# Loading in order of need, stacks read in two goes and another order of products in a four-layer attention and feed-forward kernel

## The chip, the cores and the metric

One core of one Trainium2 chip runs the whole program. The metric is the device time in microseconds (us) of one execution, median of the runs. The engines are TensorE (PE in the profile, with its weight loads as PEld), VectorE (DVE), ScalarE (ACT), GpSimd (POOL) and SyncE (SP), which here issues nearly all transfers.

## The reference

The input x is 4 batches of 512 tokens of 256 channels, the context is 4 batches of 512 tokens of 128 channels, all in 32-bit floats. Each of four layers adds a cross attention and then a feed-forward to x:

```python
x = x + _L0_xattn_ref(_layernorm(x), ctx_512, ...)   # 16 heads of 16: causal self part plus context part
x = x + _L0_ffn_ref(_layernorm(x), ...)              # ternary weights, gelu, 1024 hidden
x = x + _L1_xattn_ref(_layernorm(x), ctx_512, ...)   # 16 heads of 16
x = x + _L1_ffn_ref(_layernorm(x), ...)              # weights adapted by tokens
x = x + _L2_xattn_ref(_layernorm(x), ctx_512, ...)   # two blocks with 16 heads of 32, each with its own feed-forward
x = x + _L2_ffn_ref(_layernorm(x), ...)              # gated, two hidden layers of 1024, output
x = x + _L3_xattn_ref(_layernorm(x), ctx_512, ...)   # 16 heads of 16
x = x + _L3_ffn_ref(_layernorm(x), ...)              # 4-bit rounding of x, weights and hidden values
```

The last feed-forward is `nvfp4_linear(silu(gate) * up, down_w)`: its input and its hidden values are rounded in blocks of 16 to a 4-bit grid, each block with a scale of 8 bits.

## The kernel before

The program is written as a plan: one list of steps (`Turn`, `ProjectStack`, `ReadStack`, `Smax`, `GateUp` and others), in an order made by the Python code. Each engine's program walks that list and emits its own part of each step, so the place of a step in the list is its place on every engine that takes part in it, and on SP's queue. Waits are on semaphores; `hold` (`Hold`) makes the engines that it names wait for a list of events, and at the end of each stage all engines, SP too, wait for everything.

**Memory.** X (all tokens, 128 partitions by 16 tiles by 256) stays in the on-chip memory for the whole program. XT holds the normalised and transposed x, ctxT the transposed context, and xn is scratch: the normalised tiles, and in `load_context` (L878) the raw context too. PSUM has 8 banks of 128x512: three pairs `bank_t`, `bank_o` and `bank_m`. A `Banks` object (L62) hands them out in turn, and who takes one waits until its last reader is done. During attention the ring `misc` is `bank_m` alone.

**The start.** SP loads x (4 transfers, L254), the context (L886, 1 MB in runs of 512 bytes), the weights of L1's attention (L864), the biases of L0's feed-forward (L1085) and then L0's weights and biases (`L0_xattn`, L911). PE transposes the context for all four batches (`load_context`: 16 transposes, 4 copies by ACT), batch 0 of x is normalised into the same xn (`LazyNorm`, L334), transposed and copied, and `hold(loads)` (L929) waits for all of L0's loads.

**Attention with heads of 16** (L0, L1, L3; `attention`, L420). A unit is 8 heads of a batch; L0 has 16 units, L1 and L3 have 8. For each unit PE projects K and Q (`project_stack`, L510), ACT writes the result and a rounded high half, POOL the low half, SP spills both halves to DRAM and reads them back into the stacks `KS` and `QS` (`ReadStack`, L538 and L2581: 6 transfers of 128 KB for K, 6 for Q). A stack has 4 slots, one for a pair of heads. The first pass (`Smax`, L573) takes the scores of each pair `s` and each of 4 query tiles to find the row maxima on DVE; every `Smax` waits for the whole of both stacks. Then the maxima are turned, spilled and read into the stack as additional rows, and the second pass makes logits, exponentials and values. `chores` and `delayed` set what is done at each tick: `later(n, step)` delays a step by n ticks, `run_due` (L494) takes what is due and one chore. Unit 0 is prepared by `run_all()` before the first score; POOL fills rows of ones (`StackRest`, L798), and the statistics of the remaining batches (`norm.rest`, L800) are the first chore after it.

**The L2 feed-forward** (`L2_ffn`, L1438) goes over two pairs of batches. Weight blocks come in over SP two ahead of their use (`load_block`), are split by ACT and DVE (`split_block`: L2230, L2391, L2232) and used by PE; the output (`output`, L1526) takes 8 blocks of `w3` with all 8 banks. The 4-bit weights of the last layer are made in its background.

**The start of L3** (`L3_xattn`, L1579): after the stage's end SP loads the 4-bit weights, L3's attention weights and the context, PE transposes the context, DVE fills rows of ones (two memsets, L2133), makes batch 0's statistics and normalises it, after which PE transposes it and projects K and Q.

**The last stage** (`L3_ffn`, `main` at L1806) has 19 items of work: 3 for the x of batches 1 to 3, and 16 tiles of 128 tokens. In step k of its loop come, in plan order: `hidden_of(k + 2)` (`GateUp`: 4 groups of 2 matmuls into 4 banks, silu by ACT at L2408, the gating product by DVE at L2301); the turning of item k-2 (2 groups of 4 transposes, 2 copies by ACT at L2400, and for a tile the down product of 8 matmuls and DVE's addition to X at L2305); the block maxima of item k+1 (L2257); the grid of item k (L2284, L2286 on DVE, L2405 on ACT); the scales of item k+1 (9 small DVE instructions, L2551 on POOL); the rounding of item k (L2291, L2294 on DVE, L2559 on POOL). Its ring `f.ring` has 5 banks; a step takes 7. `end_step` carries the last steps of the attention along for k below 6.

Of the kernel before, what the change touches and what calls it, by code (L numbers as in the profile page):

```python
# [8 lines left out]
P = 128  # L9
# [80 lines left out]
ReadStack = namedtuple("ReadStack", "at un which spill after landing")  # L90
# [51 lines left out]
class Unit:  # L142
    def __init__(self, n, b, j, job, u, last):
        self.n, self.b, self.j, self.job, self.u, self.last = n, b, j, job, u, last
        self.buf, self.stacked, self.smax, self.m_in, self.raw_out = None, [], None, None, []

# [36 lines left out]
def build_program(nc, dram, out):  # L183
    ctx = ExitStack()
    with ctx:
# [68 lines left out]
        x_in = [load(X[:, TB * b:TB * b + TB, :], dram["x"][b].rearrange("(t p) c -> p t c", p=P)) for b in range(B)]  # L254
# [79 lines left out]
        class LazyNorm:  # L334
# [16 lines left out]
            def steps(self, b, ring, more=()):  # L351
# [3 lines left out]
                def normal():  # L355
# [4 lines left out]
                    if self.bias is not None:  # L360
                        row, e_row = self.bias
                        bias_added[b] = add_rows(X[:, TB * b:TB * b + TB, :], row, [self.normal[b], e_row])
# [57 lines left out]
        def attention(tag, scope, D, jobs, project, st, norm=None, following=None, side=None):  # L420
# [117 lines left out]
            def read_stack(un, which, written):  # L538
                if un.n >= st.n and un.n - st.n not in finished:
                    later(1, lambda: read_stack(un, which, written))  # L540
                    return
                at_ = landing(n=3 * st.q_of)
                add(ReadStack(at, un, which, split_dram[which][un.n % 3],
                              [written, stack_done.get(un.n - st.n), st.ready[un.buf]], at_))
                spill_read[which, un.n] = at_.done
                un.stacked.append(at_.done)
# [26 lines left out]
            def smax(un, s, qt):  # L573
# [3 lines left out]
                step = Smax(at, un, s, qt, tile, [*tiles.free[i_t], *un.stacked], mm,  # L577
# [218 lines left out]
            run_all()  # L796
            if D == 16:
                add(StackRest(st, st.ready, st.v_ones))  # L798
# [58 lines left out]
            tail.ot_free = OT_free  # L857
# [20 lines left out]
        def load_context():  # L878
            ctx_tok = xn[:, :, :, :].rearrange("p s t c -> p (s t c)").rearrange("p (t c) -> p t c", c=CC)
            e_in = load(ctx_tok, dram["ctx_512"].rearrange("b (t p) c -> p (b t) c", p=P), xn_free)  # L880
            for b in range(B):
                e_t, e_c = turn([ctx_tok[:, TB * b + i, :] for i in range(TB)], [e_in], "scalar", ctxT[:, b, :])
# [3 lines left out]
        ctx_ready = load_context()  # L886
# [24 lines left out]
        def L0_xattn(scope, keep, follows):  # L911
# [3 lines left out]
            W = {n: sb(scope, f"L0_{n}", [P, KC, C]) for n in ("Wq", "Wk", "Wv", "Wcq")}  # L915
            Wc = {n: sb(scope, f"L0_{n}", [P, 1, C]) for n in ("Wck", "Wcv")}
            bq = sb(scope, "L0_bcols", [P, 4, KC])
            rows = {n: sb(scope, f"L0_{n}", [P, C]) for n in ("bv", "bcv", "bp")}
# [3 lines left out]
            loads += [load(bq[:, i, :], dram[f"L0_xattn_{n}_cols"])  # L922
                      for i, n in enumerate(("bq", "bk", "bcq", "bck"))]
            loads += [row_load(rows[n], f"L0_xattn_{n}") for n in rows]
            norm = LazyNorm((rows["bp"], loads[-1]), lambda t: x_in[t // TB])
            for step in norm.steps(0, ALL):
                step()
            xt = norm.ready
            hold(loads)  # L929
            xsrc = lambda b: (XT[:, b, :, :], KC, xt[b])  # L930
            csrc = lambda b: (ctxT[:, b:b + 1, :], 1, [ctx_ready])
            return attention("L0", scope, 16, [
                dict(qsrc=xsrc, ksrc=xsrc, Wq=parts(W["Wq"]), Wk=parts(W["Wk"]), Wv=W["Wv"], bq=bq[:, 0, :], bk=bq[:, 1, :],
                     bv=rows["bv"], mode="causal"),
                dict(qsrc=xsrc, ksrc=csrc, Wq=parts(W["Wcq"]), Wk=parts(Wc["Wck"]), Wv=Wc["Wcv"], bq=bq[:, 2, :],
                     bk=bq[:, 3, :], bv=rows["bcv"], mode="full")], project_into(X, Wo), st, norm, follows)
# [148 lines left out]
        def L0_ffn(keep, side, norm):  # L1085
            b1, b2 = sb(keep, "L0f_b1", [P, KF]), sb(keep, "L0f_b2", [P, C])
            th = sb(keep, "L0f_th", [P, 2, 4])
            loads = [load(b1[:, :], dram["L0_ffn_b1_cols"]), row_load(b2, "L0_ffn_b2")]
            f = split_ffn(keep, "L0f", X, X, b2, b1, loads, side, exact=True)
            for b in range(2):  # L1090
# [1562 lines left out]
```

## Time and profile before

| | us |
|---|---|
| median of 3 runs | 3652.71 (3636.51 to 3660.86) |
| the profiled execution | 3634.89 |
| its span in the profile | 3633.1 |
| PE busy in the span | 2869.3 (79%) |
| DVE busy | 2040.3 (56%) |
| ACT busy | 1460.1 (40%) |
| POOL busy | 1146.9 (32%) |

The profile's times count from the start of the span. Busy time is the time in which an engine carried out an instruction; waits stand beside the instruction that came after them, with what released it. PEclk is the clock granted to TensorE as a share of the full clock.

### The profile page before, as it was taken

Reading aid. Unit: us, or ns where it says so; the run is one execution under the profiler, and the core shown is the slowest. Engines: PE = TensorE matmul, PEld = TensorE weight load, DVE = VectorE, ACT = ScalarE, POOL = GpSimd, SP = SyncE. Lnnn points to the kernel's source line nnn. Section 1 sums busy time; section 2 is a strip of 40 time slices with the busy share of each in tenths; the row PEclk is TensorE's granted clock in tenths of the full one; section 3 lists DMA queues with packets and bytes.
Section 4 is the critical chain, followed back from the end, with each engine's and each line's share of the span. In section 5 each row is a group of like instructions: output and inputs, shape, how many; then the busy total and the mean of one; then the engine's idle time right before and its main releaser. Section 6 shows DMA issues by size and latency. Waiting matters only on the chain. (4 is left out here: it accounts for less than half of the span.)

```text
span 3633.1 us, 44859 instructions
## 1 busy us (share of the span) xinstructions
PE 2869.3 (79%) x16756; PEld 1615.4 (44%) x16756; DVE 2040.3 (56%) x3607; ACT 1460.1 (40%) x1932; POOL 1146.9 (32%) x1007
## 2 busy tenths in 40 slices
PE   4888888658866979999866888877999997588544
PEld 2333333443324534444662344356778776233122
DVE  3445546756634735444784666685454443566587
ACT  1254555415551225444422545432433432266422
POOL 2122322221222225555413768650010110122333
PEclk7599989777886989999987899888999998699666
DMA  5355545024521001111100000000221221564100
GB/s 125 72 114 102 117 101 116 19 48 109 106 70 39 1 18 36 40 40 60 59 7 12 1 1 1 13 12 15 74 76 34 66 61 58 91 117 97 32 10 14
DMA packets 129176, 198.50 MB, mean 55 GB/s; under 512 B 35712, under 2 KB 65921, under 8 KB 128833
## 3 DMA queue, kind: packets, MB, share of 16 engines
q1 hardware_dynamic: 97216, 143.23, 17.4%
q0 software_dynamic: 31744, 52.41, 5.2%
q8 instruction: 134, 2.20, 0.3%
q14 instruction: 82, 0.66, 0.1%
HBM read 130.73 MB, written 64.75 MB: 54 GB/s over the span
## 5 line engine op out<-in xcount | busy, mean ns | idle before, releaser
L2148 DVE TENSOR_REDUCE L_mx<-bank_t 128x2 f32<-128x1024 f32 (+3 forms) x512 | 562.7, 1121 | 492.8 <-PE bank_t L1956 307.8
L2355 ACT ACTIVATE L_P<-bank_t 128x1024 f32<-128x1024 f32 (+2 forms) x512 | 477.9, 945 | 469.9 <-PE bank_t L1970 285.5
L2148 DVE TENSOR_REDUCE L2a_mx<-bank_t 128x2 f32<-128x1024 f32 x256 | 311.4, 1222 | 398.5 <-PE bank_t L1933 397.7
L2355 ACT ACTIVATE L2a_P<-bank_t 128x1024 f32<-128x1024 f32 x256 | 261.6, 1023 | 289.0 <-PE bank_t L1945 288.7
L1956 PE MATMUL bank_t<-L_KS,L_QS 48*128 48x512 f32 (+2 forms) x1024 | 261.7, 514 | 105.6 <-DMA L_QS<-L_spill_q_halves 84.8
L1970 PE MATMUL bank_t<-L_QS,L_KS 50*128 50x512 f32 (+2 forms) x1024 | 241.5, 476 | 108.2 <-DVE L_mx L2148 81.2
L1933 PE MATMUL bank_t<-L2a_QK 32*128 32x512 f32 x1536 | 255.9, 448 | 71.6 <-DVE L2a_mx L2148 35.5
L2001 PE MATMUL bank_o<-L_P,L_V 128*32 128x512 f32 (+3 forms) x2048 | 286.4, 636 | 2.6 <-ACT xn L2362 1.8
L1956 PEld LDWEIGHTS bank_t<-L_KS,L_QS 48*128 48x128 f32 x1024 | 107.5, 209 | 349.9 <-issue 246.5
L1941 PE MATMUL bank_t<-L2a_QK 32*128 32x512 f32 x1536 | 259.4, 447 | 0.0
L1933 PEld LDWEIGHTS bank_t<-L2a_QK 32*128 32x128 f32 x1536 | 138.0, 197 | 236.6 <-issue 105.5
L2470 POOL TENSOR_TENSOR L_lo<-L_full,L_hi 128x512 fp32r<-128x512 f32 x64 | 81.2, 1269 | 449.3 <-ACT L_hi L2342 429.7
L1895 PE MATMUL bank_t<-L2g_act_high,L2g_w_high 128*128 128x512 f32 x472 | 186.8, 396 | 18.8 <-DVE L2g_w_low L2232 16.6
L1970 PEld LDWEIGHTS bank_t<-L_QS,L_KS 50*128 50x128 f32 x1024 | 106.4, 207 | 204.5 <-DVE L_mx L2148 140.4
L2239 DVE TENSOR_TENSOR L2g_act_low<-ctxT,L2g_act_high 128x512 fp32r<-128x512 f32 x96 | 67.4, 703 | 218.2 <-ACT L2g_act_high L2396 218.2
L1895 PE MATMUL bank_t<-L2g_act_high,L2g_w_low 128*128 128x512 f32 x472 | 185.2, 392 | 0.0
L1895 PE MATMUL bank_t<-L2g_act_low,L2g_w_high 128*128 128x512 f32 x472 | 185.2, 392 | 0.0
L2480 POOL TENSOR_TENSOR L2a_sums<-L2a_sums,L2a_P 128x1024 f32<-128x1024 f32 x64 | 153.6, 2400 | 31.2 <-ACT L2a_P L2355 27.1
L2001 PE MATMUL bank_o<-L2a_P,L2a_V 128*32 128x512 f32 (+3 forms) x896 | 141.3, 566 | 1.7 <-ACT L2a_P L2355 1.7
L2475 POOL TENSOR_TENSOR L2a_diag<-L2a_P,after_q 128x256 f32<-128x256 f32 x128 | 94.9, 742 | 143.7 <-issue 80.8
L2005 PE MATMUL bank_o<-L2a_P,ones 128*32 128x512 f32 x512 | 138.0, 616 | 0.0
L1941 PEld LDWEIGHTS bank_t<-L2a_QK 32*128 32x128 f32 x1536 | 130.6, 195 | 13.8 <-issue 10.7
(424 smaller groups left out, 6057.6 us busy)
## 6 DMA issues: line engine op xcount, KB each, us to landing
L_KS<-L_spill_k_halves SPq DMA_DIRECT2D x192, 128.0 KB, 4.6
L_QS<-L_spill_q_halves SPq DMA_DIRECT2D x192, 128.0 KB, 5.2
L_spill_raw<-xn POOLq DMA_DIRECT2D x64, 256.0 KB, 2.5
L2g_raw<-in_L_ffn_h_blocks SPq DMA_DIRECT2D x32, 512.0 KB, 3.8
L_spill_k_halves<-L_hi SPq DMA_DIRECT2D x32, 256.0 KB, 2.0
L_spill_k_halves<-L_lo SPq DMA_DIRECT2D x32, 256.0 KB, 2.3
L_spill_q_halves<-L_hi SPq DMA_DIRECT2D x32, 256.0 KB, 2.5
L_spill_q_halves<-L_lo SPq DMA_DIRECT2D x32, 256.0 KB, 3.1
```

What stands on the lines that cost most here:

```text
L1895: mm = e.matmul(out_, w, x, start=first and i == 0, stop=last and i == len(terms) - 1)
L1933: mm = e.matmul(m.tile[:, c, :], Q[r, m.qt * P:(m.qt + 1) * P], K[r, :], start=i == 0, stop=i == 2)
L1941: e.matmul(l.tile[:, c, :], K[r, l.kt * P:(l.kt + 1) * P], Q[r, :], start=i == 0, stop=False)
L1956: mm = e.matmul(m.tile[:, c, 0:n_keys], st.QS[m.un.buf][rows, slot, m.qt * P:(m.qt + 1) * P], st.KS[m.un.buf][rows, slot, 0:n_keys], start ...
L1970: mm = e.matmul(x.tile[:, c, q0:S], st.KS[x.un.buf][rows, slot, x.kt * P:(x.kt + 1) * P], st.QS[x.un.buf][rows, slot, q0:S], start=True, s ...
L2001: mm = e.matmul(bank_o[row:row + 32, q0:q1], V[:, s.kt, head, :], moving, start=s.first and i == 0, stop=s.last and i == len(cuts) - 1, ti ...
L2005: mm = e.matmul(bank_o[row + 32:row + 64, :], ones[:, 0:32], s.at.Pr[pb][:, c, :], start=s.first, stop=s.last, tile_position=(0, row + 32))
L2148: e.tensor_reduce(neg, s.tile[:, :, 0:n_keys], AX.X, ALU.max, negate=True).then_inc(sem(s.done), 1)
L2355: e.activation(s.at.Pr[s.pb][:, :, q0:S], s.tile[:, :, q0:S], ACT.Exp, scale=s.at.scale).then_inc(sem(s.exp), 1)
L2470: e.tensor_tensor(s.low[:, :], s.full, s.high[:, :].bitcast(F32), ALU.subtract).then_inc(sem(s.lo), 1)
L2475: e.tensor_tensor(s.dst[:, :, :], s.src, after_q[:, :].unsqueeze(1).to_broadcast([P, 2, P]), ALU.mult).then_inc(sem(s.done), 1)
L2480: e.tensor_tensor(s.dst[:, :, :], s.a[:, :, :], s.b[:, :, :], ALU.add).then_inc(sem(s.done), 1)
```

## The change

1. x comes in batch by batch: batch 0 first, then L0's Wk, bk, Wq, bq and bp (`L0_first`). Only these are held for before batch 0 is normalised and projected. Then come batches 1 to 3, the other weights of L0, L1's weights, the biases of L0's feed-forward and the context, all after the steps for batch 0 in the list. The context is transposed in `rest`, called by `attention` (`begun`) behind the K and Q projections of unit 0, with `misc` as its ring, and L0's other loads are held for there.
2. Unit 0 of L0, L1 and L3 reads its stacks in two goes: slot 0 of K and of Q first, and a tick later slots 1 to 3. `Smax` waits for the second go only from pair 1 on.
3. In `L2_ffn` the context for L3 is fetched before the output of pair 0, and batch 0's statistics for L3 are made before the output of pair 1.
4. In the last stage a step k turns item k-2 first, then comes `hidden_of(k + 2)`, then the down product of item k-2. From k = 6 on the ring has a sixth bank, `bank_m`.

```diff
@@ start of the program
-        x_in = [load(X[:, TB * b:TB * b + TB, :], dram["x"][b].rearrange("(t p) c -> p t c", p=P)) for b in range(B)]
+        x_in = []
+
+        def fetch_x(b):
+            x_in.append(load(X[:, TB * b:TB * b + TB, :], dram["x"][b].rearrange("(t p) c -> p t c", p=P)))
+        fetch_x(0)
@@ attention
+                after = [written, stack_done.get(un.n - st.n), st.ready[un.buf]]
+                if un.n == 0:
+                    un.first_slots = 1
+                    later(1, lambda: read_slots(un, which, slice(un.first_slots, st.slots), after, un.stacked_later))
+                    read_slots(un, which, slice(0, un.first_slots), after, un.stacked)
+                else:
+                    read_slots(un, which, slice(0, st.slots), after, un.stacked)
...
-                step = Smax(at, un, s, qt, tile, [*tiles.free[i_t], *un.stacked], mm,
+                step = Smax(at, un, s, qt, tile, [*tiles.free[i_t], *un.stacked, *([] if s == 0 else un.stacked_later)], mm,
...
             chores += prep(units[0])
             run_all()
+            if begun is not None:
+                begun(misc)
@@ context
-        def load_context():
-            ctx_tok = xn[:, :, :, :].rearrange("p s t c -> p (s t c)").rearrange("p (t c) -> p t c", c=CC)
-            e_in = load(ctx_tok, dram["ctx_512"].rearrange("b (t p) c -> p (b t) c", p=P), xn_free)
+        def fetch_context():
+            return load(ctx_tok, dram["ctx_512"].rearrange("b (t p) c -> p (b t) c", p=P), xn_free)
+
+        def load_context(e_in, ring=None):
...
-        ctx_ready = load_context()
+        ahead = {}
@@ L0
+        def L0_first(scope):
+
+            f = Stage()
+            f.W = {n: sb(scope, f"L0_{n}", [P, KC, C]) for n in ("Wq", "Wk")}
+            f.bq, f.bp = sb(scope, "L0_bcols", [P, 4, KC]), sb(scope, "L0_bp", [P, C])
+            f.loads = [weight_load(f.W["Wk"][:, :, :], "L0_xattn_Wk", KC), load(f.bq[:, 1, :], dram["L0_xattn_bk_cols"]),
+                       weight_load(f.W["Wq"][:, :, :], "L0_xattn_Wq", KC), load(f.bq[:, 0, :], dram["L0_xattn_bq_cols"])]
+            f.e_bp = row_load(f.bp, "L0_xattn_bp")
+            return f
...
+            norm = LazyNorm((first.bp, [first.e_bp]), lambda t: x_in[t // TB])
+            for step in norm.steps(0, ALL):
+                step()
+            xt = norm.ready
+            hold(first.loads)
+            bq, ctx_ready = first.bq, []
+
+            for b in range(1, B):
+                fetch_x(b)
             loads = [weight_load(W[n][:, :, :], f"L0_xattn_{n}", KC) for n in W]
...
+            w.fetch()
+            follows.fetch()
+            e_ctx = fetch_context()
+
+            def rest(ring):
+                ctx_ready.append(load_context(e_ctx, ring))
+                hold(loads)
@@ L2_ffn and L3_xattn
                 if pair == 0:
                     e_x = turned_pair(e_normal, e_mm)
+                    ahead["context"] = fetch_context()
+                else:
+                    ahead["norm"] = LazyNorm(None)
                 e_out = output(pair, act[0], [e_h])
...
-            e_ctx = load_context()
-            norm = LazyNorm(None)
+            e_ctx = load_context(ahead["context"])
+            norm = ahead["norm"]
@@ last stage (down returns out_of, which makes the down product; turn_x returns a step that does nothing)
                 def end_step(k):
                     if k < 6:
                         tail.tick()
-                    elif k == 6:
+                    elif k == 6 and len(f.ring.aps) == 5:
                         tail.rest()
+                        f.ring.aps.append(ALL.aps[7])
+                        f.ring.free.append(tail.misc.free[0])
...
                 for k in range(len(work)):
-                    hidden_of(k + 2)
-                    end_step(k)
+                    finish = lambda: None
                     if k >= 2:
                         turn_it, rounded = turning.pop(0)
-                        turn_it(*rounded)
+                        finish = turn_it(*rounded)
+                    end_step(k)
+                    hidden_of(k + 2)
+                    finish()
                     end_step(k)
```

## Rows read from the trace of the kernel before

**Rows 1.** Windows by stage: busy us (instructions) per engine, PEclk, DMA share, GB/s.
```profile
0.00:51.20 51.20, 10.50 (x32) 5.99 (x32) 9.36 (x27) 6.80 (x10) 16.23 (x23) 0.76 0.75 174
...
3410.00:3633.00 223.00, 98.48 (x424) 50.88 (x424) 182.48 (x389) 59.13 (x91) 79.20 (x45) 0.62 0.05 14
```

**Rows 2.** Timeline from 0 to 60 us: start, length, engine, line, out<-in, [idle before].
```profile
4.02 5.10 SPq L2576 DMA_DIRECT2D L_Wq<-in_L_xattn_Wq  x1
5.33 1.40 DVE L2076 BATCH_NORM_STATS2 stats<-X 128x6 f32<-128x256 f32 x4
...
9.38 0.16 DVE L2099 SCALAR_TENSOR_TENSOR rstd<-nw 128x4 f32<-128x4 f32 x1
...
12.95 3.67 PE L1906 MATMUL bank_t<-ident,xn 128*128 128x128 f32 x16 [12.95 <-DMA xn<-in_ctx]
...
16.73 1.38 DVE L2106 TENSOR_SCALAR xn<-X,mv,rstd 128x256 f32<-128x256 f32 x4 [7.20 <-PE bank_t L1906]
...
25.65 3.75 PE L1895 MATMUL bank_m<-XT,L_Wk 128*128 128x512 f32 x4 [6.38 <-DMA L_bp<-in_L_xattn_bp]
...
34.43 1.26 POOL L2470 TENSOR_TENSOR L_lo<-L_full,L_hi 128x512 fp32r<-128x512 f32 x1 [2.05 <-ACT L_hi L2342]
...
39.50 2.77 SPq L2589 DMA_DIRECT2D L_QS<-L_spill_q_halves  x6
51.27 0.48 PE L1956 MATMUL bank_t<-L_KS,L_QS 48*128 48x128 f32 x2 [18.37 <-DMA L_QS<-L_spill_q_halves]
...
53.55 4.01 DVE L2076 BATCH_NORM_STATS2 stats<-X 128x6 f32<-128x256 f32 x12
...
57.94 0.33 PE L1956 MATMUL bank_t<-L_KS,L_QS 48*128 48x128 f32 x2
```

**Rows 3.** Timeline, the start of L1's attention.
```profile
771.87 2.77 SPq L2589 DMA_DIRECT2D L_QS<-L_spill_q_halves  x6
782.31 1.65 PE L1956 MATMUL bank_t<-L_KS,L_QS 48*128 48x512 f32 x6 [17.20 <-DMA L_QS<-L_spill_q_halves]
```

**Rows 4.** Timeline, the start of L3's attention.
```profile
3066.83 1.76 DVE L2133 MEMSET L_KS<- 32x2048 f32 x1 [0.47 <-issue]
3066.97 0.44 SPq L2576 DMA_DIRECT2D L_Wv<-in_L_xattn_Wv_T  x1
...
3083.74 1.68 PE L1895 MATMUL bank_m<-ctxT,L_Wk 128*128 128x512 f32 x2
...
3095.43 2.77 SPq L2589 DMA_DIRECT2D L_QS<-L_spill_q_halves  x6
3107.61 1.65 PE L1956 MATMUL bank_t<-L_KS,L_QS 48*128 48x512 f32 x6 [18.77 <-DMA L_QS<-L_spill_q_halves]
```

**Rows 5.** DMA issues, 3060 to 3110 us: count, size, median us to landing.
```profile
L_spill_k_halves<-L_hi SPq DMA_DIRECT2D x1, 256.0 KB, 2.0
...
L_Wv<-in_L_xattn_Wv_T SPq DMA_DIRECT2D x1, 128.0 KB, 6.4
```

**Rows 6.** Timeline of DVE, block scaling in the outputs of pair 0 and pair 1.
```profile
2776.82 0.42 DVE L2230 TENSOR_TENSOR L2g_raw<-L2g_raw,ctxT 128x256 f32<-128x256 f32 x1
...
3036.06 0.42 DVE L2230 TENSOR_TENSOR L2g_raw<-L2g_raw,ctxT 128x256 f32<-128x256 f32 x1
```

**Rows 7.** DVE's waits, 3410 to 3633 us: us in total, times, longest.
```profile
DVE X L2305 <- PE bank_t L1895: 13.7, 8, 4.9
DVE X L2305 <- PE bank_o L1895: 4.4, 4, 1.3
```

**Rows 8.** Timeline, one step of the last stage.
```profile
3538.35 0.48 DVE L2305 SCALAR_TENSOR_TENSOR X<-bank_o,L3f_cols,X 128x256 f32<-128x256 f32 x1 [1.33 <-PE bank_o L1895]
...
3542.28 1.25 ACT L2408 ACTIVATE L3f_hid<-bank_t,L3f_cols 128x512 f32<-128x512 f32 x2
...
3546.07 1.40 DVE L2301 SCALAR_TENSOR_TENSOR L3f_hid<-bank_t,L3f_cols,L3f_hid 128x512 f32<-128x512 f32 x2
...
3548.80 0.48 DVE L2305 SCALAR_TENSOR_TENSOR X<-bank_t,L3f_cols,X 128x256 f32<-128x256 f32 x1 [1.33 <-PE bank_t L1895]
```

More of the change, by code:

```diff
@@ L89 @@
 SpillStack = namedtuple("SpillStack", "at s spill after landing")
-ReadStack = namedtuple("ReadStack", "at un which spill after landing")
+ReadStack = namedtuple("ReadStack", "at un which slots spill after landing")
 ProjectValues = namedtuple("ProjectValues", "at un t0 n bank after mm")
@@ L418, in fill_stacks, with attention @@
             add(StackInit(st, st.ready))
-        def attention(tag, scope, D, jobs, project, st, norm=None, following=None, side=None):
+        def attention(tag, scope, D, jobs, project, st, norm=None, following=None, side=None, begun=None):
             H, NU = st.H, HEADS // st.H
@@ L921, in L0_xattn @@
             loads += [weight_load(Wo[:, :, :], "L0_xattn_Wp", KC)]
-            loads += [load(bq[:, i, :], dram[f"L0_xattn_{n}_cols"])
-                      for i, n in enumerate(("bq", "bk", "bcq", "bck"))]
+            loads += [load(bq[:, i, :], dram[f"L0_xattn_{n}_cols"]) for i, n in ((2, "bcq"), (3, "bck"))]
             loads += [row_load(rows[n], f"L0_xattn_{n}") for n in rows]
[L925 to L929, printed above, removed]
+            w.fetch()
[4 more added lines that the diff above has]
+                hold(loads)
             xsrc = lambda b: (XT[:, b, :, :], KC, xt[b])
-            csrc = lambda b: (ctxT[:, b:b + 1, :], 1, [ctx_ready])
+            csrc = lambda b: (ctxT[:, b:b + 1, :], 1, ctx_ready)
             return attention("L0", scope, 16, [
-                dict(qsrc=xsrc, ksrc=xsrc, Wq=parts(W["Wq"]), Wk=parts(W["Wk"]), Wv=W["Wv"], bq=bq[:, 0, :], bk=bq[:, 1, :],
-                     bv=rows["bv"], mode="causal"),
+                dict(qsrc=xsrc, ksrc=xsrc, Wq=parts(first.W["Wq"]), Wk=parts(first.W["Wk"]), Wv=W["Wv"], bq=bq[:, 0, :],
+                     bk=bq[:, 1, :], bv=rows["bv"], mode="causal"),
                 dict(qsrc=xsrc, ksrc=csrc, Wq=parts(W["Wcq"]), Wk=parts(Wc["Wck"]), Wv=Wc["Wcv"], bq=bq[:, 2, :],
-                     bk=bq[:, 3, :], bv=rows["bcv"], mode="full")], project_into(X, Wo), st, norm, follows)
+                     bk=bq[:, 3, :], bv=rows["bcv"], mode="full")], project_into(X, Wo), st, norm, follows, begun=rest)
         def norm_x(src=None, evac=None, ready=never, **more):
@@ L1857, in main @@
                 for then, rounded in turning:
-                    then(*rounded)
+                    then(*rounded)()
             f.loads, f.steps, f.main = lambda st, e_free: [], steps, main
@@ L1863, in build_program @@
         with ExitStack() as outer:
-            w = L1_weights(outer)
-            norm, side = LazyNorm((w.bo, w.loads[-1]), lambda t: out_ready[t], False), Side()
-            attention_and_ffn(L0_xattn, lambda keep: L0_ffn(keep, side, norm))
+            first, w = L0_first(outer), L1_weights(outer)
+            norm, side = LazyNorm((w.bo, w.loads), lambda t: out_ready[t], False), Side()
+            attention_and_ffn(lambda scope, keep, follows: L0_xattn(scope, keep, follows, first, w),
+                              lambda keep: L0_ffn(keep, side, norm))
             assert not side.items
@@ L2588, in sync_program @@
                             row = st.part * q + D * r
-                            e.dma_start(stack[row:row + D, :, :].bitcast(F32), halves[q]).then_inc(sem(s.landing.done), 16)
+                            e.dma_start(stack[row:row + D, s.slots, :].bitcast(F32),
+                                        halves[q][:, s.slots, :]).then_inc(sem(s.landing.done), 16)
                 elif kind is RowsOut and s.landing is not None:
```

40 lines of the change are left out of this document (24 added, 16 removed).

## The prediction, made before the changed kernel had run

> **What bounds the kernel now.** Read first the busy time by stage [rows 1]. In the first 51.2 us PE works for 10.5 us and DVE for 9.4, while the DMA engines are busy for 0.75 of the time: the start is bound by transfers and by the order in which they come. In the last 223 us DVE works for 182.5 and PE for 98.5: that stage hangs on DVE. Between these the attention and feed-forward stages are not touched, apart from the starts of L1 and L3 and the two outputs of the L2 feed-forward.
>
> Then the timeline of the start [rows 2] shows which wait ends last at each step. Batch 0's statistics run from 5.33 to 9.54, but its normalisation starts at 16.73, since PE has to turn the context out of the shared xn first, and that came in at 12.95. The K projection starts at 25.65 and was held for bp, the last of all loads. The low half of Q is done at 35.69 (34.43 + 1.26), the reads of the Q stack are issued by 42.27 (39.50 + 2.77), and the first score starts at 51.27, 9.0 us after. L1 has 7.7 us in that place (774.64 to 782.31) [rows 3] and L3 has 9.4 (3098.20 to 3107.61) [rows 4]. In the last stage read DVE's waits: PE's down product holds it up 12 times for 18.1 us [rows 7], and one step shows how: 1.33 us of waiting in a period of 10.45 (3538.35 to 3548.80) [rows 8].
>
> **A, L0's loads in order of need.** DVE still gets to batch 0's statistics at 5.33, and rstd is there at 9.54. With no context in xn the normalisation follows at once: 1.38 us, to 10.9 [rows 2]. The 16 context transposes took 3.67 us at the start, so 8 take 1.84; with a copy of about 0.7 and some 0.3 of handing over, XT is complete at 13.8. Wk, bk, Wq and bq are issues 2 to 5 of SP's queue, behind 512 KB only, and a load issued among many lands 6.4 us after issue [rows 5], so by about 10: they are not late. The K projection starts at 13.8 in place of 25.65, a gain of **11.9**. From there to the end of Q's low half takes 10.0 us as before (25.65 to 35.69), so to about 23.8.
>
> SP has 22 more issues (three of x, nine of L0, eight of L1, two of L0's feed-forward are 22, then the context) at 0.46 us each (2.77 for 6), so it is through at about 15. But the transfer issued right behind the context held SP for 5.10 us before [rows 2]; now that would be the spill of K, and 15 + 5 = 20 is just when K's low half is ready. All 6 MB of loads were in by about 25 before, and some 22 to 24 now; the context is the last of them. Its turning now stands on PE's queue in front of the first score, with one bank: 4 times (4 transposes 0.92 + copy 0.6 + handing over 0.3) = 7.3 us, from about 24 to 31.5. The stacks' reads cover it until 32.5; past that each us costs one.
>
> **B, stacks in two goes.** The first go has the same 12 issues as the whole read had, with a quarter of the bytes, so it is issued as early as before. Before, 1.5 MB had to pass, and the last landed 9.0, 7.7 and 9.4 us after its issue; a spill on an idle queue lands in 2.0 [rows 5]. Bounds for the wait after the last issue: 2.0 from below, the old 9.0, 7.7 and 9.4 from above. I take 2.2, by the row of the idle queue, since 32 KB transfers leave no backlog: gains 6.8 + 5.5 + 7.2 = **19.5**. The second go is 12 issues more, 5.5 us of SP, which has nothing else to do there; it is issued by 47.8 on the old time scale and lands by 50 to 51.3. The first score of pair 1 came 6.7 us after the first of all (51.27 to 57.94) [rows 2], so now at 44.5 + 6.7 = 51.2. It just fits, and should it be late by 1 or 2 us, DVE covers it, which then makes 12 tiles' statistics (4.01 us from 53.55, and the root after them) before it takes the next maxima. Cost taken: 0, at most 2 per stage.
>
> The Trainium skill (DMA: Bandwidth & Descriptors, section Bandwidth) speaks against this part: transfers under 64 KB are dominated by their descriptors, and about 2 us per transfer are fixed whatever its size. If that stood for each of 12 transfers one after the other, the first go would take some 25 us, an estimate by that page. The trace bears the fixed time out but not its adding up: the row of one spill has 2.0, and 12 reads are in within 15 us.
>
> **C, L3's start.** The context is in xn when the stage begins, and the statistics are made. DVE's second memset ends at 3068.59 [rows 4]; normalisation 1.38, transposes 1.84, copy and handing over 1.0 give XT at 3072.8. The weights are then late: Wv is issued at 3066.97 with 0.44 and lands 6.4 after [rows 4, 5], 3073.4 to 3073.8. The K projection starts at 3073.7 in place of 3083.74: a gain of **10.0**. If 4 context turns (3.7 us from 3064) or the weights were 2 us slower, it is 8.
>
> **D, what C moves into the L2 feed-forward.** Four statistics and the root, 4.2 us on DVE (5.33 to 9.54 [rows 2]), now stand ahead of the scaling of block 1 at 3036.06 [rows 6], whose split PE needs one block later. DVE has room between its blocks, PE's block takes part of it: from 0 to 4.2, I take 2. In pair 0 the context (1 MB) goes into SP's queue ahead of the load of a block that is scaled at 2776.82 [rows 6], and SP waits for PE's turning of xn first. Lower bound 0, upper bound the 5.1 us for which the issue behind the context hung before [rows 2]; I take 1, since blocks are loaded two ahead. Cost **3**.
>
> **E, the last stage.** Before, the four banks of `hidden_of`, two of turning and one of down followed each other in a ring of 5, so the down product waited for a bank that DVE's gating of the same step had to free; then DVE waited for the product. Now the order is T1, T2, four gate and up banks, down. Counting back 5, each takes a bank whose reader came a step earlier, but for the last gate group (T1's copy) and down (T2's copy, which it needs anyway). The product is done before DVE asks. Nine waits of 1.33 go: the 12 waits less three of another size (4.9 at the end of the kernel, 0.8 and 0.5), gain **12.0** of 18.1. What is late next is the silu: the two copies (1.2) now come first, so two silus that ran from 3542.28 for 1.25 end at 3544.7; DVE takes them at 3546.07 [rows 8]. 1.4 us are left, so DVE alone sets the step: 9.1 us. The sixth bank then gives nothing, 0 (bounds 0 and 1). The first six steps, which carry the attention's end, may shift by 3 either way; the drain behind the last item stays.
>
> **Sum.** 11.9 + 19.5 + 10.0 - 3 + 12.0 = 50.4, say 50. The profiled execution took 3634.9 (span 3633.1 and 1.8 around it): 3585. It was the fastest of what is shown; the median, 3652.7, is 0.5% higher. If the change's runs lie about theirs in the same way, the median is **3602**.
>
> **The rivals.**
> 1. The start is late: SP hangs behind the context, or the context lands after 26, and its turning stands in front of the scores. For it: the 5.10 [rows 2]. Against: SP is idle when it happens. A loses 10: gain 40, 3612. Chance 0.10.
> 2. Small transfers land no sooner: the stack reads are slow per transfer (12 took 14.6 us), and a quarter of the bytes takes nearly as long. B gives 0 in place of 19.5: gain 31, 3622, within 1%. Chance 0.12. Its hard form is the page's rule read in series: the first goes take 25 us where whole stacks took 14.6, 10 lost in each of three stages, gain 1 and 3652; of the 0.12 I give it 0.02.
> 3. The silu holds DVE, so E gives nothing: the margin of 1.4 is gone if PE's work at the turn comes late. Gain 38, 3614. Chance 0.06.
> 4. Slower: turning first puts a wait ahead of the gate products. If the rounded item k-2 is not there when PE reaches it, the turning (0.6), copies (1.2), gate and up products (about 3.4 at PE's pace there) and silu (0.7) run in series behind DVE's rounding, 5.9 us in each of 16 steps, 94 in all. With the 38 gained elsewhere that is 3634.9 + 56 = 3691, 3709 as median. It decides from 2.4 us a step on (38 / 16). Against it: the item was rounded two steps back, and the period of 10.45 has DVE at work for 9.1, with PE idle for more than half of the stage [rows 1]. Chance 0.04.
>
> **How the numbers follow.** The forecast has 0.68, with 8 us to either side of 50 from its unknown terms (B by 3, D by 4, A and C by 3, E by 3), and runs of one kernel differ by up to 0.7% here. A measurement of this kernel tells about 1%, 36.5 us. The forecast passes it in 0.66, rival 1 in 0.06, rival 3 in 0.04 and rival 2 in 0.01: faster 0.77. Slower by over 1% is rival 4 with 0.04, and 0.19 is left for no difference. Its own range, 3594 to 3610, is widened by how runs scatter and by rivals 1 to 3: 3574 to 3630.
>
> **What would show it.** The K projection at 13 to 15 us; the first score at 31 to 34; the reads in goes of 12 with the first score 2 to 3 us after the twelfth; 5 to 6 us less between Q's spill and the scores in L1; L3's K projection 10 us earlier against the end of the stage before; no 1.33 at the additions to X, and steps of 9.1. Wrong would be: waits of `Smax` for the second go above 2 us, a hole in the L2 outputs above 5, a first score held by the turned context, or DVE waiting at L2301 for ACT in each step.

## The result and the profile after

The changed kernel takes 3600.81 us (median of 4 runs, 3582.92 to 3610.70), the kernel before 3644.61 (4 runs); the ratio is 0.9886 with a 95% interval of 0.985 to 0.9922. The forecast was 3602 and faster by over 1%: that it is faster is shown, that it is by over 1% is likely and not shown, since the interval begins at 0.8%. The profiled execution has a span of 3602.4 us (3633.1 before), 30.7 less: 11 us less of a gain than the ratio gives, and 19 less than the sum of the prediction (50). The first question is therefore where the steps' gains stand, and only then the total.

First the timeline of the changed kernel's start (start, length, engine, line, out<-in, [idle before]), which answers to [rows 2]:

```profile
13.84 3.75 PE L1949 MATMUL bank_m<-XT,L_Wk 128*128 128x512 f32 x4 [0.87 <-DVE XT L2165]
...
16.77 0.84 SPq L2630 DMA_DIRECT2D xn<-in_ctx  x1
...
19.11 3.64 PE L1949 MATMUL bank_m<-XT,L_Wq 128*128 128x512 f32 x4 [1.51 <-ACT L_hi L2396]
...
24.82 0.66 PE L1960 MATMUL bank_m<-ident,xn 128*128 128x128 f32 x4 [2.07 <-DMA xn<-in_ctx]
...
26.50 2.73 SPq L2643 DMA_DIRECT2D L_KS<-L_spill_k_halves  x6
...
29.28 2.74 SPq L2643 DMA_DIRECT2D L_QS<-L_spill_q_halves  x6
...
33.55 0.47 PE L2010 MATMUL bank_t<-L_KS,L_QS 48*128 48x128 f32 x2 [2.67 <-DMA L_QS<-L_spill_q_halves]
...
34.86 2.76 SPq L2643 DMA_DIRECT2D L_QS<-L_spill_q_halves  x6
...
42.53 0.33 PE L2010 MATMUL bank_t<-L_KS,L_QS 48*128 48x128 f32 x2 [2.33 <-DMA L_QS<-L_spill_q_halves]
...
43.17 3.01 DVE L2202 TENSOR_REDUCE L_mx<-bank_t 128x2 f32<-128x768 f32 x4
```

The K projection starts at 13.84 in place of 25.65, the first score at 33.55 in place of 51.27, 1.53 us behind the twelfth read of the first go (29.28 + 2.74) where it was 9.0. Pair 1 waits 2.33 us for the second go, but that is hidden: DVE takes pair 1's maxima at 43.17, 9.6 us behind the first score, and it was 9.6 before too (60.89 against 51.27), because the statistics of 12 tiles stand between.

The starts of L1 and L3 answer to [rows 3, 4]. In L3 the line to look at is Q's projection, 3.74 us long (1.98 before):

```profile
760.50 2.73 SPq L2643 DMA_DIRECT2D L_QS<-L_spill_q_halves  x6
...
764.75 1.65 PE L2010 MATMUL bank_t<-L_KS,L_QS 48*128 48x512 f32 x6 [10.80 <-DMA L_QS<-L_spill_q_halves]
...
3061.01 0.33 SPq L2630 DMA_DIRECT2D L3f_GT<-L3f_gate_fp  x1
...
3070.35 2.05 PE L1949 MATMUL bank_m<-ctxT,L_Wk 128*128 128x512 f32 x2 [1.32 <-DMA L_Wv<-in_L_xattn_Wv_T]
...
3073.83 3.74 PE L1949 MATMUL bank_m<-XT,L_Wq 128*128 128x512 f32 x4 [1.44 <-ACT L_hi L2396]
...
3084.09 2.73 SPq L2643 DMA_DIRECT2D L_QS<-L_spill_q_halves  x6
...
3088.35 1.65 PE L2010 MATMUL bank_t<-L_KS,L_QS 48*128 48x512 f32 x6 [10.77 <-DMA L_QS<-L_spill_q_halves]
```

In the outputs of the L2 feed-forward, which answer to [rows 6], DVE's waits (us in total, times, longest) in pair 0's output show a late block, and SP's show why. Before, the first of these lines read 0.8 us, once:

```profile
DVE L2g_raw L2284 <- DMA L2g_raw<-in_L_ffn_w_blocks: 4.3, 2, 3.4
```
```profile
SPq L59 <- PE bank_t L1960: 9.8, 1, 9.8
```

In the last stage (DVE's waits from 3393 us to the end, which answers to [rows 7], and one step, to [rows 8]) the waits for the down product are gone but for the three of another size:

```profile
DVE L3f_hid L2355 <- ACT L3f_hid L2462: 12.9, 2, 11.6
DVE X L2359 <- PE bank_t L1949: 5.4, 2, 4.9
DVE X L2223 <- PE bank_m L1949: 3.8, 1, 3.8
...
DVE X L2359 <- PE bank_m L1949: 0.4, 1, 0.4
```
```profile
3514.67 0.47 DVE L2359 SCALAR_TENSOR_TENSOR X<-bank_o,L3f_cols,X 128x256 f32<-128x256 f32 x1
...
3519.55 1.27 ACT L2462 ACTIVATE L3f_hid<-bank_t,L3f_cols 128x512 f32<-128x512 f32 x2
3519.80 1.69 PE L1949 MATMUL bank_m<-L3f_DT,L3f_hq 128*128 128x256 bf16 x8
...
3522.38 0.74 DVE L2355 SCALAR_TENSOR_TENSOR L3f_hid<-bank_t,L3f_cols,L3f_hid 128x512 f32<-128x512 f32 x1
...
3523.69 0.47 DVE L2359 SCALAR_TENSOR_TENSOR X<-bank_m,L3f_cols,X 128x256 f32<-128x256 f32 x1
```

A step takes 9.02 us (3514.67 to 3523.69) where it took 10.45. The down product ends at 3521.49, 2.2 us before DVE asks for it. One wait is new, 3.8 us before the attention's last addition to X (L2223). It is no loss: the kernel before waited 5.06 us for a silu at that place, the changed one 3.8 and then 1.31.

So each step stands nearly where it was forecast. What is missing lies between them. To see it, the same points are marked in every profile, and each is compared in time with the same point in the profile of before: how much earlier it comes is its lead. The start of the spill of the row maxima marks each of the 32 units of the three attentions with heads of 16, and the first scaling of pair 0's output marks L2. The lead over the first profile of the kernel before, in us:

| mark | changed kernel | the same, second profile | kernel before, second profile |
|---|---|---|---|
| L0 unit 0 | 17.6 | 17.2 | -0.9 |
| L0 unit 4 | 26.3 | 25.1 | 11.0 |
| L0 unit 15 | 11.2 | 31.2 | -7.5 |
| L1 unit 0 | 17.7 | 37.7 | -6.4 |
| L1 unit 1 | 11.1 | 30.0 | -7.2 |
| L1 unit 7 | 15.2 | 23.4 | -5.0 |
| L2, pair 0's output | 8.2 | 21.3 | -14.6 |
| L3 unit 0 | 21.2 | 34.4 | -14.5 |
| L3 unit 7 | 17.0 | 31.3 | -18.4 |
| last addition to X | 30.7 | 43.8 | -17.8 |

The table holds two things. Leads wander by 10 to 20 us inside stages that the change does not touch. And one loss is the same in both profiles with the change: 6.6 and 7.7 us between units 0 and 1 of L1.

### The profile page after: what moved, and what is told of

The parts are those of the page before. It is cut to its first block and busy times, and to the rows that moved or that the text cites. A ratio compares the mean times of both kernels' runs of the same rounds, so it can differ in the third digit from the quotient of the medians.

```text
span 3602.4 us, 44895 instructions
## 1 busy us (share of the span) xinstructions
PE 2886.6 (80%) x16756; PEld 1623.2 (45%) x16756; DVE 2034.1 (56%) x3607; ACT 1460.1 (41%) x1932; POOL 1147.6 (32%) x1007
## 3 DMA queue, kind: packets, MB, share of 16 engines
q1 hardware_dynamic: 97792, 143.23, 17.3%
## 5 line engine op out<-in xcount | busy, mean ns | idle before, releaser
L2534 POOL TENSOR_TENSOR L2a_sums<-L2a_sums,L2a_P 128x1024 f32<-128x1024 f32 x64 | 153.7, 2401 | 29.2 <-ACT L2a_P L2409 25.1
```

Of the source, the lines that this page charges most:

```text
L2534: e.tensor_tensor(s.dst[:, :, :], s.a[:, :, :], s.b[:, :, :], ALU.add).then_inc(sem(s.done), 1)
```

## The experiments

Two questions: is the wandering the chip's or the change's, and what does each part bring alone. "Only" means the kernel before with that part alone, its code as in the diff above.

**The two kernels once more, unchanged.**

> The kernel before, unchanged, once more. Theory (the clock is drawn anew in each execution): the ratio is 1.00 within 0.3%, and set against the first profile of before the starts of the same steps drift apart by 5 to 15 us within stages bound by PE, in both directions, with the granted clock of those windows different. Rival (the clock is a function of the program): the drift stays under 2 us everywhere, and then the 6.5 us that the changed kernel loses between its unit 0 and unit 10 are the change's own doing.

> The changed kernel, unchanged, once more. Both theories: ratio 0.986 to 0.991, first score at 33.5. Theory (clock drawn anew): the gain against before at unit 9 of L0 is not 11.1 again but anything from 5 to 25. Rival (a denser start draws a lower clock later): 17.6 at unit 0 and again 11.1 from unit 9 on.

Measured: 0.9989 (0.9957 to 1.0021) for the kernel before against itself, 0.9889 (0.9854 to 0.9924) for the change. The leads are the table's second and third columns. Without any edit the kernel before drifts from 11.0 ahead to 18.4 behind. Where it drifts, the granted clock differs. The clearest place is between the row maxima of L0's units 4 and 5, the same work of the same kernel, where the second profile takes 6.2 us more (window, its length, PE's busy time and count, PEclk, DMA share, GB/s), first the first profile of the kernel before, then its second:

```profile
252.74:286.55 33.81, 31.29 (x206) 1.00 0.55 114
```
```profile
241.76:281.80 40.04, 38.46 (x208) 0.80 0.47 96
```

PE is busy for 31.29 us at the full clock and for 38.46 at 0.80 of it, for the same matmuls (206 and 208 on record). The drift is drawn anew in each execution, so one profile's span says nothing of an effect under 20 us; a difference must be read between neighbouring marks, or from many runs.

**The last stage alone, the stacks in two goes alone.**

```diff
+                        finish = turn_it(*rounded)
+                    end_step(k)
+                    hidden_of(k + 2)
+                    finish()
```


> Only the order of the last stage and the sixth bank. Theory: from the last row maxima of L3 to the end of the span 12 to 14 us less than in before, steps of 9.0, total 0.9965 (12.5 of 3645 less). Rival (E is worth less than its waits, since PE's clock falls with its busy time there): below 8 us.

Measured: 0.9949 (0.992 to 0.9978); from L3's unit 7 to the last addition the lead goes from -11.1 to +2.0, 13.1 us (13.7 and 12.5 in the two profiles of the whole change). The rival falls by that stretch; the ratio alone, 8 to 29 us, would not have told.

```diff
+                if un.n == 0:
+                    un.first_slots = 1
```


> Only the stack reads of unit 0 in two goes. Theory: the first score follows the last issue of its go by 1.5 to 2.5 us in L0, L1 and L3, where before had 9.0, 7.7 and 9.4; gains 7, 6 and 7.5 at the first score, and 1 to 4 us of that are given back at pair 1, which waits for the second go; total 15 to 19 us, 0.9955. Rival (part B is taken back wholly by the wait for the second go): the third row maxima of unit 0 come no more than 2 us earlier, total 0.999 to 1.0.

Measured: 0.9936 (0.9909 to 0.9963). The first scores stand 1.5 us behind the last issue of their go in all three stages. In L0 the lead at the first score is only 4.5, since in this execution bp landed 1.4 later and Q's projection took 3.78, with the order of loads of before; L1's start brings 6.5, and L3's 8.2, read at the statistics of the next batches. Next to nothing is given back at pair 1: the lead at unit 0's maxima is still 4.2. In kernels without this part the wait from the last issue to the first score varies in L1: 5.6, 5.8, 6.9, 7.6 and 7.7 us in five runs, and 7.7 in the first profile of before.

**The loads of L0 alone.**

```diff
+            hold(first.loads)
+            bq, ctx_ready = first.bq, []
```


> Only L0's order of loads and the early start. Theory: K projection at 13.8 as in the changed kernel, and Q's projection takes 3.6 to 3.8 in place of 1.98, because PE no longer has the context's transposes in front of it; Q's reads are issued by 32 in place of 42.3, so 10.2 us of gain and not 11.9; first score 8 to 9 after the last issue, at 40 to 41; total 0.997. Rival (the slow Q projection is a draw of that execution only): 1.98 here, and 12 us.

Measured: 1.0001 (0.9974 to 1.0028). The part brings nothing, though its first score is at 40.59 and its lead at unit 0's maxima is 10.1. And the theory on Q's projection falls: it took 1.98 here, and the reads of Q's stack were issued no earlier than with 3.64. SP's lines show what holds them:

```profile
17.48 0.84 SPq L2623 DMA_DIRECT2D xn<-in_ctx  x1
20.30 1.76 SPq L2626 DMA_DIRECT2D L_spill_k_halves<-L_hi  x1
22.11 0.43 SPq L2627 DMA_DIRECT2D L_spill_k_halves<-L_lo  x1
...
26.79 2.67 SPq L2636 DMA_DIRECT2D L_KS<-L_spill_k_halves  x6
29.50 2.77 SPq L2636 DMA_DIRECT2D L_QS<-L_spill_q_halves  x6
```
```profile
SPq L2636 <- DMA L_spill_k_halves<-L_lo: 2.3, 1, 2.3
```

K's spill goes out behind the context and lands 4.7 us after its issue, at 26.8 (2.0 in [rows 5]). Whichever is later, this landing or Q's projection at its slow length, sets the reads to 26.5 or 26.8.

The 10 us are lost in L1. From unit 0's row maxima to unit 1's it takes 48.2 us, where before took 36.0, with the steps of L1 unchanged; the same unit 1 waits 9.8 us for its stack in place of 6.5, and unit 0's second pass 6.15 for its maxima in place of 1.02.

**L3's context and statistics alone, and the context fetched later.**

```diff
+                    ahead["context"] = fetch_context()
+                else:
+                    ahead["norm"] = LazyNorm(None)
```


> Only L3's context and statistics ahead. Theory: in the output of pair 0 the third block is scaled 2.5 to 3 us later than without the context (its load stands behind the context's on SP's queue), in pair 1 the second block 1 us later; L3's K projection 9.5 after the stage's first transfer where before had 19.7; Q's projection 3.7 in place of 1.98; net at L3's first score 10.2 - 1.8 - 3.8 = 4.6. Total 0.9987, no difference that can be measured. Rival (the 2.9 us lost in the output of pair 0 were the clock of that execution): the loss is not there, net 8 or more.

Measured: 0.9983 (0.996 to 1.0005). In pair 0's output the third block is 4.1 late, 2.5 are still lost at the last block; in pair 1's 1.0. The K projection comes 9.6 after the stage's first transfer (19.7 before), Q's takes 3.78, and the last of Q's reads is issued 26.2 after it in place of 34.1: 7.9 gained for 3.5 lost. The slow projection isn't the part's alone: in the run of only A, whose L3 starts as before, it takes 3.78 too.

```diff
-                    ahead["context"] = fetch_context()
...
+                if pair == 1:
+                    ahead["context"] = fetch_context()
                 e_mm, e_h = layer(xs, KC, e_x, act[0], [e_out], None, "gated")
```


> The changed kernel, but the context for L3 is fetched at the begin of pair 1's first layer in place of before pair 0's output. Theory (the context's load stands in the way of blocks that PE uses up in 2.9 us each): DVE's wait of 3.4 for a block in pair 0's output goes, the output takes 2.7 to 2.9 us less, nothing is lost in the layer, where a block lasts PE over 10 us. Rival (the wait is for SP, held until PE has turned xn): the same wait comes back in the layer.

One run, 3620.22 us. The lead is -1.5 at the first block of pair 0's output and -1.5 at the last: nothing is lost there, as the theory has it, against 1.5 to 2.5 in the six profiles that fetch the context before that output. But the gain does not last. From the first block of pair 0's output to the last of pair 1's the lead falls by 5.1 here, and by 4.7 to 5.7 in those six (5.1 and 5.0 in the changed kernel's two profiles). Of the six profiles without part C three lose 4.1 or 4.2 over the same stretch and three nothing, so how much of it is the drift is open; that the later place of the fetch is worth its 2 us is not shown. DVE's wait there is again that of before:

```profile
DVE L2g_raw L2285 <- DMA L2g_raw<-in_L_ffn_w_blocks: 0.7, 1, 0.7
```

**PE kept at work before the start.** `Warm` is a step of 30 transposes of `ident` into bank_m.

```diff
+            add(Warm(bank_m, [const_ready], 30))
             for step in norm.steps(0, ALL):
```


> The changed kernel with 30 transposes of the constant identity matrix into the idle bank_m before batch 0's, from 3.5 to about 10.5 us; their result is used by nothing. Theory (PE's matmuls at the start are slow because PE was idle before them): batch 0's 8 transposes take 1.1 in place of 1.97, K's projection 1.98 in place of 3.75, Q's 1.98 in place of 3.64; the first score comes 3.5 to 4.3 us earlier, at 29.3 to 30.1, unless the context's landing (24.8) and turning hold it. Rival (the start is slow whatever PE did before): no change.

One run, 3595.36 us. The projections are as fast as the theory has it, but the first score comes 0.6 earlier and not 3.5 to 4.3:

```profile
3.55 5.09 PE L1962 MATMUL bank_m<-ident 128*128 128x128 f32 x30 [3.55 <-POOL ident L2496]
11.01 1.09 PE L1966 MATMUL bank_t<-ident,xn 128*128 128x128 f32 x8 [2.36 <-DVE xn L2166]
12.97 1.95 PE L1951 MATMUL bank_m<-XT,L_Wk 128*128 128x512 f32 x4 [0.88 <-DVE XT L2171]
16.44 1.98 PE L1951 MATMUL bank_m<-XT,L_Wq 128*128 128x512 f32 x4 [1.51 <-ACT L_hi L2402]
...
18.00 3.12 SPq L2639 DMA_DIRECT2D L_spill_k_halves<-L_hi  x1
...
32.93 0.47 PE L2016 MATMUL bank_t<-L_KS,L_QS 48*128 48x128 f32 x2 [1.69 <-DMA L_QS<-L_spill_q_halves]
```

The spill's issue comes right behind the context now and holds SP for 3.12 us, and lands 7.2 after it began. The start of the changed kernel is bound by its transfers from 18 us on. Two later kernels say the same: Q's projection took 1.98 in their start (the last two runs below) and their first scores stand at 33.37 and 34.38, where the changed kernel had 33.55 and 33.70.

**Why part A is paid back in L1.** The part changes nothing of L1's steps, but its first weights are allocated in an outer scope, so L1's tiles and the stacks of L0 lie 5,152 bytes further in each partition of the on-chip memory (two weights of 2,048 bytes, biases of 32 and 1,024). That can be done alone, and undone alone.

```diff
         with ExitStack() as outer:
+            for n, c in (("Wq", KC * C), ("Wk", KC * C), ("bcols", 4 * KC), ("bp", C)):
+                sb(outer, f"pad_{n}", [P, c])
             w = L1_weights(outer)
```


> The kernel before, with 5,152 bytes per partition of on-chip memory taken and not used ahead of L1's weights: all tiles of L0 and L1 lie where the changed kernel has them, nothing else differs. Theory (part A is paid back in L1 because its tiles lie elsewhere, and the reads of units 1 and 2 then land slower): from unit 0's row maxima in L1 to unit 1's 42 to 48 us, as in the five profiles with part A, and PE's wait for unit 0's maxima over 5 us. Rival (it is drawn in each execution): 36 to 37 us and 1.0 to 1.7, as in four of the five profiles without part A.

One thing in this is not exact: by the order of allocation, L0's tiles that come behind those biases are moved by the padding and not by the change. For L1, where the loss is, the two agree.

> The changed kernel with the loads of before: parts B, C, D and E alone. Theory (A's 10 us at the start are given back in L1): total 0.988 to 0.990, as the whole change, and 36 us between the row maxima of L1's units 0 and 1. Rival (A's gain stays, and the run of A alone fell badly): 10 us slower than the whole change, 0.991 to 0.993.

In the next diff the added call stands in `L0_xattn`, behind `fill_stacks`.

```diff
-            first, w = L0_first(outer), L1_weights(outer)
+            w = L1_weights(outer)
...
+            first = L0_first(scope)
```


> The changed kernel whose first weights are allocated in L0's own scope, as before, so that L1's tiles lie where they lay; order of loads and all else as in the change. Theory of the place in memory: 36 us between the row maxima of L1's units 0 and 1, total 0.986 to 0.987, 7 to 9 us below the changed kernel's. Rival (the place does not matter): 42 to 48 us there, total 0.989.

Measured: the padded kernel (one run, 3653.04 us) takes 41.0 us between the maxima of L1's units 0 and 1, 1 less than the theory's 42 to 48, with a wait for unit 0's maxima of 5.06 as it says; the change without A 35.7, the change with its weights in the inner scope 35.7. PE's two waits for DMA in that stretch, kernel before, padded, and inner scope:

```profile
825.24 1.65 PE L1956 MATMUL bank_t<-L_KS,L_QS 48*128 48x512 f32 x6 [6.50 <-DMA L_QS<-L_spill_q_halves]
...
832.56 0.79 PE L1970 MATMUL bank_t<-L_QS,L_KS 50*128 50x512 f32 x2 [1.02 <-DMA L_QS<-L_spill_max_rows]
```
```profile
822.12 1.65 PE L1958 MATMUL bank_t<-L_KS,L_QS 48*128 48x512 f32 x6 [8.71 <-DMA L_QS<-L_spill_q_halves]
...
833.48 0.79 PE L1972 MATMUL bank_t<-L_QS,L_KS 50*128 50x512 f32 x2 [5.06 <-DMA L_QS<-L_spill_max_rows]
```
```profile
791.08 1.65 PE L2011 MATMUL bank_t<-L_KS,L_QS 48*128 48x512 f32 x6 [5.81 <-DMA L_QS<-L_spill_q_halves]
...
799.31 0.80 PE L2025 MATMUL bank_t<-L_QS,L_KS 50*128 50x512 f32 x2 [1.93 <-DMA L_QS<-L_spill_max_rows]
```

The transfers are the same; the moved tiles keep the DMA engines busy for 0.46 of the stretch in place of 0.34, and the reads of unit 2's Q stack, behind which the maxima's reads are queued, land 7.1 us after issue in place of 3.6 (medians of six). Totals: 0.987 (0.9823 to 0.9917) without A, so no loss is seen by leaving A out, though the interval would hide one of 10 us; 0.9834 (0.9791 to 0.9876), 3589.68 us, with A in the inner scope, the lowest ratio of all. The interval overlaps that of the changed kernel, so that this version is faster than the change is likely and not shown; that it is faster than before is.

**Is it the 32 bytes?** The move is no multiple of 64 bytes. The next kernel makes it one; its third edit, not printed here, is the later fetch of the context, as above.

```diff
-            f.bq, f.bp = sb(scope, "L0_bcols", [P, 4, KC]), sb(scope, "L0_bp", [P, C])
+            f.bq, f.bp = sb(scope, "L0_bcols", [P, 8, KC]), sb(scope, "L0_bp", [P, C])
...
+            sb(keep, "L3_pad", [P, 8])
             st = make_stacks("L3", 16, keep, 8)
```


> The changed kernel with three edits. The first weights stay where the change puts them, but the tile of 32 bytes of biases takes 64, so that all stacks of L0 and L1 begin 5,184 bytes further than in before and at a multiple of 64 (in the change and in the padded kernel 5,152 further, at 32 past one). 32 unused bytes ahead of L3's stacks, which lie at 32 past a multiple of 64 in every kernel so far. And L3's context is fetched at the begin of pair 1's first layer. Theory (the 32 bytes decide): 36 us between the row maxima of L1's units 0 and 1 and 185 to 195 from there to unit 7's; in L3 under 38.7 between the first two. Rival (the distance moved or the neighbourhood decides, not the 32 bytes): 41 to 48 in L1. Context: the third block of pair 0's output is no longer late (2.9 us). Total by the theory 0.982 to 0.985, by the rival 0.987 to 0.989.

Measured: 43.1 between the first two units of L1, and 38.8 in L3 as in nearly all others. The theory of the 32 bytes falls, the rival stands: it is where the tiles lie, not their offset in 64. The context fetched later again costs nothing in pair 0's output (26.2 ahead at its first block and at its last), and again 5.1 us are gone by the last block of pair 1's. Total 0.9847 (0.9815 to 0.9878), 3580.35 us, lower than the rival's 0.987 to 0.989; how much of it is the context's place and how much the draw isn't told apart.

All profiles together, in us between row maxima, the moved ones being those with part A in the outer scope or with padding:

| | L1, unit 0 to 1 | L1, unit 1 to 7 | L0, unit 0 to 15 |
|---|---|---|---|
| tiles as before, 7 profiles | 35.6 to 37.1, and 40.5 once; mean 36.8 | 184.0 to 194.3, mean 189.2 | 523.9 to 543.2, mean 532.5 |
| tiles moved, 7 profiles | 41.0 to 48.2, mean 44.2 | 185.9 to 206.5, mean 195.6 | 513.6 to 540.1, mean 522.6 |

The first column does not overlap. But the one 40.5 (only C, tiles as before) is within 0.5 us of the lowest moved profile, and it looks like them inside: PE waits 8.62 us for unit 1's stack and 4.20 for unit 0's maxima, where the other six unmoved profiles have 5.8 to 7.2 and 1.0 to 1.9, and the seven moved ones 8.6 to 9.8 and 5.1 to 6.6. So the place makes the slow transfers likely and isn't their only way. The other two overlap and stay open: the move may cost L1 6 us more and may bring L0 10.

## Why the prediction was right or wrong

The total was met to 1 us, and partly by luck. By its own steps:

- **A, start of the K projection:** forecast a gain of 11.9, measured 11.8. The context's landing and turning, forecast 24 to 31.5, measured 24.8 to 31.5, and in front of no score. The failed part of the step is "to the end of Q's low half takes 10.0 us as before": it took 11.7 (13.84 to 25.54), as Q's projection ran at 3.64 us. That does not come with the part every time: in the six profiles with part A and no added transposes it took 3.4 to 3.8 in three and 1.98 in three. At the last issue of Q's reads the gain is 10.2 (42.27 to 32.02). Q's speed alone would not have saved it: with 1.98, K's spill landed too late. That is rival 1 in a mild form: SP was held behind the context for 1.76 and 3.12 us where the spill came early.
- **A, what the step did not have:** the place of L1's tiles. It takes 7.4 us back (44.2 - 36.8). A alone measured 1.0001; a gain of 10 would be 0.9973, just outside its interval, one of 3 is inside.
- **B:** forecast a wait of 2.2 behind the last issue, measured 1.5 in each stage; gains 7.5, 6.2 and 7.9, in sum 21.6 for 19.5. The lower bound of 2.0, from a spill of 256 KB, was too high for reads of 32 KB. L1's 6.2 is set against a wait of 7.7; against the 5.6 of another execution it is 4. The second go came 2.3 (L0) and 4.0 us (L1 and L3) late where "it just fits" was forecast. Over 2 us was named as a sign of being wrong, and it came; the step held because DVE covered it as said. Rival 2 falls. The Trainium skill's rule (DMA: Bandwidth & Descriptors, section Bandwidth) that transfers under 64 KB are dominated by their descriptors costs nothing here: the twelve of 32 KB overlap, and the last is in 1.5 us after its issue.
- **C:** forecast 10.0, measured 10.3 at the K projection (19.66 to 9.34 behind the stage's first transfer), and 8.3 at the last issue of Q's reads (34.12 to 25.81), again by Q's projection, 3.74 in place of 1.98.
- **D:** forecast 3, the context 1 and the statistics 2. Measured 2.0 at the last block of pair 0's output (8.2 to 6.2) and 1.0 in pair 1's: the sum right, its halves exchanged, by the outputs' own marks; whether the 2.0 is a loss at all is open, as fetching later did not bring it back (the run of the later fetch). The wait has the forecast's mechanism, SP held 9.8 us by PE's turning with the context next in its queue, but "since blocks are loaded two ahead" was no cover: a block of this output lasts PE 2.9 us.
- **E:** forecast 12.0 and steps of 9.1, measured 13.1 alone and steps of 9.02. The silu does not hold DVE in a step (the gating product at 3522.38 has no wait), so rival 3 falls; that the waits for ACT fell from 17.3 to 12.9 says less, since 3.8 of it now stand at L2223; the order T1, T2, gate and up, down never starved, so rival 4 does. The sixth bank was not tried alone.

The steps measured sum to 10.2 + 21.6 + 8.3 - 3.0 + 13.1 = 50.2, for 50.4 forecast. Less the 7.4 of L1 that is 42.8; the ratio gives 0.0114 x 3644.6 = 41.5 (28 to 55). The failed step of the total is the base: the sum was set against a median of 3652.7 that more runs moved to 3644.6, and this 8 stood in for the 7.4 that L1 took back. For a base of 3644.6 the same steps would have given 3594, still in the range. The total can't confirm this account, since 50.2 lies within 28 to 55 too: the loss in L1 is shown by the marks and the moved tiles, not by the total.

The clock's part is seen in the granted clock at Q's projection in L3, first of the changed kernel, then of before (the first window of the latter holds the end of K's projection, the second Q's):

```profile
3070.00:3072.00 2.00, 1.65 (x2) 0.50 0.00 0
3074.00:3076.00 2.00, 2.00 (x3) 0.50 0.00 0
```
```profile
3084.00:3086.00 2.00, 1.42 (x2) 0.74 0.00 0
3086.00:3088.00 2.00, 1.14 (x3) 1.00 0.00 0
```

At half clock, 1.2 GHz, four matmuls of 512 columns take 3.74, at full clock, 2.4 GHz, 1.98. Before, PE turned the context and batch 0 from 3076.78 on with one pause of 1.55 us and projected K right behind them; with the context turned ahead it pauses for 2.81 and, before K, for 1.32. With part C the projection took 3.5 to 3.8 in all eight profiles, without it 1.98 in five of six; the sixth, 3.78 in the run of only A, has the order of before and pauses of 1.55 and 0.98. So the part makes the half clock there likely and does not alone decide it. In L0's start, in the kernel that keeps PE at work from 3.55 us, K's projection takes 1.95. The Trainium skill (TensorE: Matmul & The Clock Gate, part 1) says that the array's clock is halved when it has been idle; these rows agree. One warning on reading the clock: in the changed kernel's start, under K's projection of 3.75 us, PEclk reads 1.00, so there the length tells the clock:

```profile
14.00:16.00 2.00, 2.00 (x3) 1.00 1.11 337
```

## What to carry to other kernels

Work that PE does while it would wait may not be free to remove: the next matmuls on the path may run at half clock, and the transfers that they feed may be late anyway, so find both covers before the gain is counted. A part that only adds a tile moves every tile behind it; when a part gains at its own place and nothing in the total, compare neighbouring marks through the whole program, and move the tiles alone. And where the same kernel wanders by 18 us between executions, a part worth 10 is read between marks, never from a span.

## What the runs showed of the hardware that was not expected

- The place of tiles in the on-chip memory changes how fast the same transfers land: 5,152 bytes further on, six reads of Q's stack land 7.1 us after issue in place of 3.6, and the stretch between two units takes 41.0 us in place of 36.0 (seven profiles with moved tiles 41.0 to 48.2, seven without 35.6 to 40.5); 5,184 bytes on it is 43.1. Which neighbourhood does it stays open.
- A burst of twelve reads of 32 KB needs no longer than its issues (5.5 us) and 1.5 us more; with 128 KB each it was 7.7 to 9.4 us more, and 5.6 at the least in other executions of L1.
- Thirty transposes on a constant, 5.09 us of a PE that was idle, bring K's projection behind them from 3.75 to 1.95 us (one run); in the six profiles of the same start without them it took 3.4 to 3.8.
